# Three sums over partitions in a fused attention and feed-forward layer: matmuls with ones, or transposes that VectorE adds up

## The reference

```python
def _L0_attn_ref(hidden_states, ...):          # hidden_states is the layer norm of x
    x = hidden_states @ up_w.T
    final_gate = hidden_states @ gate_w.T
    shift = silu(causal_conv(x, conv_w) + conv_b)
    q = shift @ q_w.T
    k = shift @ k_w.T
    v = sigmoid(x @ ig_w1.T @ ig_w2.T + ig_b2) * x
    g_gate = softplus(shift @ g_w.T + g_b)
    tau = sigmoid(shift @ tau_w.T + tau_b)
    it_gate = g_gate ** tau
    rt_log = -g_gate * tau
    kn = k / jnp.maximum(jnp.linalg.norm(k, axis=-1, keepdims=True), EPS_K) * it_gate
    o = gla_chunk_scan(q * SCALE, kn, v, rt_log)
    o = o + shift * residual_weight
    xg = o * jax.nn.silu(final_gate)
    rms = jax.lax.rsqrt(jnp.mean(xg * xg, axis=-1, keepdims=True) + NORM_EPS)
    return (xg * rms * norm_weight) @ down_w.T

def _L0_ffn_ref(x, ...):
    h = silu(lin(x, w1)) * lin(x, w2)          # 256 -> 1024
    h = gelu(lin(h, h1))                       # 1024 -> 1024
    h = gelu(lin(h, h2))
    return lin(h, w3)                          # 1024 -> 256
```

## Time and profile before

| | us |
|---|---|
| median of three runs | 1988.01 (1987.57 to 1988.39) |
| span of the profiled execution | 1984.5 |
| PE busy | 1967.8 (99%) |
| DVE busy | 1576.1 (79%) |
| ACT busy | 1258.2 (63%) |
| POOL busy | 68.6 (3%) |

### The profile page before, as it was taken

The page is one execution under the profiler, slowest core; times in us unless marked ns, Lnnn a source line. Parts: engine busy times, 40 slices in busy tenths (PEclk is TensorE's granted clock), DMA queues, the critical chain, the costliest instruction groups (busy, mean ns, idle before and its releaser), DMA issues.

```text
span 1984.5 us, 46801 instructions
## 1 busy us (share of the span) xinstructions
PE 1967.8 (99%) x17508; PEld 1954.0 (98%) x17508; DVE 1576.1 (79%) x4242; ACT 1258.2 (63%) x2495; POOL 68.6 (3%) x104
## 2 busy tenths in 40 slices
PE   7999999999999999999999999999999999999998
PEld 7999999999999999999999999999999999999998
DVE  7787778877788887787877788777888777878777
ACT  5665656666566666566656566665667665666565
POOL 0000000000000000000000000000000000000000
PEclk9999999999999999999999999999999999999999
DMA  8000000000000000000000000000000000000000
GB/s 302 7 12 12 12 7 6 12 12 12 12 1 12 12 12 12 12 1 12 12 12 12 7 6 12 12 12 12 1 12 12 12 12 12 1 12 12 12 7 7
DMA packets 23360, 34.22 MB, mean 17 GB/s; under 512 B 2945, under 2 KB 19713, under 8 KB 23186
## 3 DMA queue, kind: packets, MB, share of 16 engines
q1 hardware_dynamic: 23186, 31.46, 4.7%
HBM read 23.07 MB, written 8.39 MB: 16 GB/s over the span
## 4 chain that ended last, share of the span: by engine, by line
PE 94%; issue 2%; DVE 2%; ACT 1%; SPq 1%; DMA 0%; POOLq 0%; POOL 0%; DVEq 0%; ACTq 0%
PE fb L363 62%; PE ab L363 24%; PE ab L567 2%; PE ab L508 1%; PE ab L433 1%; PE ab L497 1%; PE fb L648 1%; PE ab L560 0%; SPq L271 0%; PE ab L559 0%; DVE hid0l L937 0%; DMA small<-stage_w 0%; ACT raw L801 0%; PE ab L558 0%; SPq L276 0%
## 5 line engine op out<-in xcount | busy, mean ns | idle before, releaser
L363 PE MATMUL fb<-hid1h,wwhole 128*128 128x256 f32 x2048 | 473.7, 279 | 0.2 <-DVE hid1l L854 0.2
L363 PE MATMUL fb<-hid1l,wwhole 128*128 128x256 f32 x2048 | 468.6, 276 | 0.0
L363 PE MATMUL fb<-hid0l,wwhole 128*128 128x256 f32 x2048 | 465.9, 276 | 0.0
L363 PE MATMUL fb<-hid0h,wwhole 128*128 128x256 f32 x2048 | 465.8, 276 | 0.0
L363 PEld LDWEIGHTS fb<-hid1h,wwhole 128*128 128x128 f32 x2048 | 384.7, 188 | 2.6 <-issue 0.4
L363 PEld LDWEIGHTS fb<-hid1l,wwhole 128*128 128x128 f32 x2048 | 384.7, 188 | 0.0
L363 PEld LDWEIGHTS fb<-hid0h,wwhole 128*128 128x128 f32 x2048 | 384.5, 188 | 0.0
L363 PEld LDWEIGHTS fb<-hid0l,wwhole 128*128 128x128 f32 x2048 | 384.4, 188 | 0.0
L801 ACT ACTIVATE raw<-fb,sh_s 128x256 f32<-128x256 f32 x512 | 213.0, 467 | 111.5 <-PE fb L363 110.6
L363 PE MATMUL fb<-xntl,wwhole 128*128 128x256 f32 x1024 | 237.5, 276 | 0.0
L363 PE MATMUL fb<-xnth,wwhole 128*128 128x256 f32 x1024 | 237.5, 276 | 0.0
(11 more groups left out here) (210 smaller groups left out, 4597.7 us busy)
## 6 DMA issues: line engine op xcount, KB each, us to landing
xin<-x SPq DMA_DIRECT2D x32, 256.0 KB, 2.7
out<-xin SPq DMA_DIRECT2D x32, 256.0 KB, 2.2
stage_more<-stage_w SPq DMA_DIRECT2D x6, 512.0 KB, 7.4
sgate<-stage_w SPq DMA_DIRECT2D x4, 512.0 KB, 4.7
shift<-stage_w SPq DMA_DIRECT2D x4, 512.0 KB, 5.2
v<-stage_w SPq DMA_DIRECT2D x4, 512.0 KB, 5.6
raw<-stage_w SPq DMA_DIRECT2D x3, 512.0 KB, 6.3
mixed<-stage_w SPq DMA_DIRECT2D x3, 512.0 KB, 8.6
```

The lines of the kernel that those rows point to most:

```text
L363: mm = pe.matmul(o, a, b, start=start and i == 0, stop=stop and i == len(pairs) - 1)
```

## The change

The matmuls with ones become transposes with the identity that lies in SBUF already. Each result has 128 columns in place of two or one, and DVE adds them up by `tensor_reduce` along the free dimension: for the scores, one reduce of 256 columns in four groups of 64 gives both sums of both chunks; for the mean square, one reduce of 256 columns in two groups of 128. Each reduce signals a semaphore of its own, on which the next DVE instruction waits. The copy of `qk_sum` and the four memsets of `pair_ones` fall away.

```diff
-        pair_ones = sb("pair_ones", [P, NC])
...
-        qk_sum = sb("qk_sum", [P, NC])
+        sums, total = sb("sums", [P, 2 * NC]), sb("total", [P, NC])
+        k_sum, qk_sum = sums[:, 0:NC], sums[:, NC:2 * NC]
...
+        sums_d, total_d = sig("sums_d", 1), sig("total_d", 1)
...
-                pe.matmul(ab[3][:, N:N + NC], t4, pair_ones[:], start=True, stop=True)
-                pe.matmul(ab[3][:, N + NC:N + 2 * NC], qk, pair_ones[:], start=True, stop=True)
+                pe.transpose(ab[3][:, N:N + P], t4, ident_s[:])
+                pe.transpose(ab[3][:, N + P:N + 2 * P], qk, ident_s[:])
...
-                    mm = pe.matmul(fb[1][:, c:c + 1], sqsum[:, c * CH:(c + 1) * CH], ones[:, 0:1], start=True, stop=True)
+                    mm = pe.transpose(fb[1][:, c * P:(c + 1) * P], sqsum[:, c * CH:(c + 1) * CH], ident_s[:])
...
-                    for c in range(NC):
-                        for col in range(NC):
-                            dve.memset(pair_ones[rows(c), col:col + 1], float(c == col))
...
-                dve.tensor_copy(qk_sum[:], ab[3][:, N + NC:N + 2 * NC])
-                dve.tensor_scalar(ssk[:], ab[3][:, N:N + NC], KEPS2, None, ALU.max).then_inc(ss_d.sem, 1)
+                dve.tensor_reduce(sums[:], ab[3][:, N:N + 2 * P].rearrange("p (s k) -> p s k", k=K), mybir.AxisListType.X,
+                                  ALU.add).then_inc(sums_d.sem, 1)
+                dve.wait_ge(sums_d.sem, sums_d.at(me))
+                dve.tensor_scalar(ssk[:], k_sum, KEPS2, None, ALU.max).then_inc(ss_d.sem, 1)
...
-                dve.tensor_scalar(msq[:], fb[1][:, 0:NC], 1.0 / DI, EPS, ALU.mult, ALU.add).then_inc(msq_d.sem, 1)
+                dve.tensor_reduce(total[:], fb[1][:, 0:NC * P].rearrange("p (c k) -> p c k", c=NC), mybir.AxisListType.X,
+                                  ALU.add).then_inc(total_d.sem, 1)
+                dve.wait_ge(total_d.sem, total_d.at(me))
+                dve.tensor_scalar(msq[:], total[:], 1.0 / DI, EPS, ALU.mult, ALU.add).then_inc(msq_d.sem, 1)
```

## The result

The changed kernel takes 1993.19 us (median of 10 runs, 1992.95 to 1994.17), the kernel before 1987.95 us in the same session (1986.91 to 1990.19). The ratio is 1.0027, with a 95% interval of 1.0019 to 1.0036: slower by 5.2 us, where 6.2 us less were forecast. The profiled executions are 7.9 us apart: 1992.4 against 1984.5.

What follows compares the result with a forecast made beforehand. TensorE, busy 99% of the span, was taken as the bound; -4.5 - 1.8 + 0.0 + 0.3 - 0.2 = -6.2 us from the median 1988.01 gave 1981.8 us, 0.31% faster. The range was 1977.5 to 1985.5.

Steps and rivals of the forecast that it cites:

- How near the chain is: VectorE and ScalarE's chain to the fourth `hid1l`, ending 0.14 and 0.21 us before TensorE's k = 6 load; hand-over 0.12.
- the room: Slack at k = 6 of the second hidden layer, capping TensorE's savings since the up projection: 0.02 us (p = 0), 0.09 (p = 1).
- (1): RMS sum at each half's end: two transposes replace two 32-bit matmuls, 0.145 us saved each, 4.5 us in all.
- (2): Two sums at the scores: TensorE 0.12 to 0.22 us earlier, capped by the room to 1.8 us in all.
- (3): VectorE at the scores: reduce of 256 columns takes 0.42 us, `att` is 0.07 late, nothing moves.
- (4): VectorE at the RMS sum: reduce and wait ahead of `msq`, free in 31 halves, +0.34 us once at the end.
- (5): Four memsets at the start go, with TensorE waiting for VectorE's flag there: -0.2 us.
- (B): Rival: VectorE's reduce runs at the strided pace, 0.61 us, delaying the fourth `hid1l`; 1984.6 us, chance 0.15.
- (C): Rival: sign turns, reduce out of PSUM dearer than either row, delaying the fourth `hid1l`; up to 1999.8 us, chance 0.05.
- (D): Rival: a transpose is not cheaper than a one-column matmul on TensorE, nothing saved; 1988.1 us, chance 0.04.
- (A): Rival: the room at k = 6 isn't that small, so all of (2) counts, 5.4 us; 1978.2 us, chance 0.13.
- (E): Rival: TensorE's clock falls to 1.2 GHz around transposes, +14 us at 64 sites; 1996 us, chance 0.02.

Runs made afterwards that it cites:

- e4: Changed kernel with TensorE taking the high parts of k = 6 and 7 in the second hidden layer before waiting for the last low parts; ratio 1.0006 to the kernel before.
- g1: Kernel before with only VectorE's reduce and wait of the score change put ahead of `ssk`; ratio 0.9999 to the kernel before.
- g2: Changed kernel's TensorE work, with VectorE reading two columns at the scores as before, without the sums; ratio 1.0022 to the kernel before.
- e3: Changed kernel with one more transpose, never read, behind the two at the scores; ratio 1.0009 to the kernel before.
- g4: Changed kernel with one more 32-bit matmul of one column behind the two score transposes; ratio 1.0028 to the kernel before.
- f1: Changed kernel with two 64-column matmuls, weights of 16 columns, ahead of the second hidden layer; ratio 0.9992 to the kernel before.
- f4: Kernel before with pairs of small matmuls, weights of 16 columns, ahead of the projections, second hidden layer and third layer; ratio 1.0133, 2014.4 us.
- h1: Kernel before with two short matmuls ahead of the second hidden layer and its high parts taken first at k = 6 and 7; ratio 1.0055.
- h3: Changed kernel with three already met waits added ahead of the second hidden layer; ratio 1.0013 to the kernel before.
- e1: Kernel before with only the RMS sum and its `msq` changed, score sums left as 32-bit matmuls; ratio 0.9989 to the kernel before.
- h4: Changed kernel with the two score transposes moved behind the matmul `kx`; ratio 1.0031 to the kernel before.
- h2: e1 with two short matmuls ahead of the second hidden layer and its high parts taken first at k = 6 and 7; ratio 1.0035.

## Why the prediction was wrong

**What bounds the kernel.** Right: TensorE's own time set the end in every kernel, and the changed kernel has one listed wait of 0.2 us, as in the earlier trace rows. The sentence that failed stands in the same paragraph: "what PE is spared comes off it, as long as no wait opens". It took the time of a matmul as the same whatever goes before it. It isn't: what went before decides between 0.1134 and 0.1178 us for the next 90. The trace of before shows it for whoever takes the same stretch in both halves: the third layer takes 3.63 us in one half and 3.77 in the next. I had read four transposes and three matmuls at the earlier trace rows and taken 0.113 for all, so the spacing of the other matmuls stood at nothing in the sum, and it measured +14.3 us.

**How near the chain is.** Right in p = 0: the wait came, 0.06 us, with a hand-over of 0.11 to 0.12 as in the earlier trace rows. In e4, where the load at k = 6 needn't wait, it begins 0.06 us after the end of the fourth `hid1l`, 0.08 sooner than the 0.14 of the earlier trace rows; 0.08 less the room of 0.02 is the 0.06 of waiting. Wrong in p = 1: no wait came, as the slow spacing had taken 0.09 us before k = 6, and the rest is less than the room. Wrong in its price: I let a wait cost its length, and in ten of the p = 0 halves it costs seven times that, since the spacing behind it is slow. The half of the earlier trace rows could have told me: its 96 matmuls took 11.65 us against 10.88, and the wait was 0.46 of the 0.77. I read the wait's end there and not what followed. (In g1 the same half has the same wait and returns to fast.)

**(1) RMS sum.** Right: 0.34 to 0.22 for the sum, 0.15 and 0.13 with the matmuls behind it, against 0.145.

**(2) Scores.** Right in size, 0.12 where 0.12 to 0.22 was given; the cap at the room was the wrong reason to count little of it. It isn't lost to the wait but bought back at four times its price by the spacing.

**(3) and (4) VectorE.** Right. The reduces take 0.418 and 0.425 us against 0.42, `ssk` follows 0.04 us behind, and the fourth `hid1l` starts right behind its ScalarE input. At the end `msq` starts 0.97 us after the load of the last sum, where it was 1979.32 - 1978.67 = 0.65: 0.32 later against 0.34. The kernel with part (3) alone took 0.9999 of the time before. The note on PSUM that (3) drew from the Trainium skill speaks of matmuls, not of VectorE's reads; the value rested on the rows. **(5)** The preparation's last matmuls start 0.2 us sooner (50.32 for 50.53 us), as forecast.

**The rivals.** (B), (C) and (D) fell with these rows. (A) wanted no wait in either half: it was so in p = 1, for another reason. (E) looked at the clock around the transposes: it is 1.00 in the window from 1000 to 1130 us with all of them in it. The Trainium skill's rule ("TensorE: Matmul & The Clock Gate", Part 4), by which transposes don't count as activity for the clock as matmuls do, changed nothing in the loop here. The clock did fall, but at 51 us, behind the preparation, and in kernels of both kinds. The mechanism that turned the sign was none of the five. The sign turned on a cost of 4.5 ns a matmul; 15106 of the 17508 records are matmuls of that kind, 256 columns on 128 columns of weights.

**The sum.** By the forecast -4.5 - 1.8 + 0.3 - 0.2 = -6.2 us. Measured over the 31 halves of the loop, by the starts of the weight loads: -4.8 at the RMS sum and z and -3.7 at the scores, savings of 8.5; +10.3 in the 96 matmuls of the second hidden layer, +2.0 in the third layer and +2.0 in the down projection, 14.3 for which the forecast had no term; +0.4 elsewhere, most of it a first hidden layer that ran slow once. That is +6.3 in this execution.

## What stays open

What makes a stretch leave the slow spacing was not found. Shown is that the loss comes with TensorE's work and not with VectorE's (g1, g2), that stretches without a wait do the same in nearly all pairs of halves of a kernel, that short work ahead can turn one either way (e3, g4, f1, f4, h1), and that added waits of the sequencer hardly turn it (h3, p = 1). Stretches behind a wait vary from one pair to the next. The first hidden layer is such a stretch in the p = 0 halves: it runs slow in one of them in the changed kernel, in six in e1, three in e3 and every third in h4, and the first load of the projections ahead of it comes 0.165 to 0.183 us behind the load before it, where it comes after 0.110 in the p = 1 halves, a wait of some 0.06 us. It can also reach far: the third layer and the down projection of the p = 0 halves are fast, but for the seven halves whose first hidden layer had run slow (six in e1, one in h1), in all five kernels whose score sums are 32-bit matmuls and that have no added pair ahead of the third layer (before, e1, g1, h1, h2), and slow in all kernels with transposes there, some 20 us of matmuls earlier, whether the second hidden layer between them is fast or slow. That small offsets in time carry this is my reading; no run set an offset on purpose. The starts of the weight loads at the projections speak for it. Where the step to the first load was 0.182 or 0.183 us and the next 0.167 or 0.168, the first hidden layer ran slow in all nine halves (six in e1, two in f1, one in h3); at 0.175 and 0.169 or 0.170 it did in all eight (three in e3, five in h4); at 0.177 or 0.178 and 0.170, as in 14 of the 15 p = 0 halves of the kernel before, in none of 23. That is a pattern of a few ns found across kernels afterwards, and no experiment.

## What to carry to other kernels

Where one engine is busy all the time, time the untouched stretches of its work before and after a change, not only the instructions that are changed: differences of starts along the chain of work show in one view whether equal matmuls still take equal time. Look for that in the trace of before too, by comparing the same stretch in different iterations; if it has two durations, a small change ahead of it can pick the other, and a forecast needs that as a rival of its own. A wait of some 0.05 us in a full stream can cost several times its length, so reordering to avoid it (the high parts first) can be worth more than the wait. Both have to be measured in the kernel at hand: the same reordering with the same short pair, put on the kernel before, cost 14.5 us (h1).

## What the hardware showed that I had not expected

Matmuls of 256 columns with a weight load each have two steady spacings at a granted clock of 1.00, 0.1134 and 0.1178 us, each held for a whole stretch of 128 matmuls in h4. The Trainium skill ("TensorE: Matmul & The Clock Gate", Part 2, Back-to-back issue gap) says that loads and matmuls together set the spacing in such a stream, and gives 256 / 2.4 + 2.5 = 109.2 ns for a matmul alone; both measured values lie above that.

Two 32-bit transposes in a row take 0.22 us with their loads, two 32-bit matmuls with one column 0.34. VectorE adds 256 contiguous 32-bit columns out of PSUM in 0.418 to 0.425 us, while the strided reduce of the earlier trace rows takes 2.0 us for 1024.

In eight of the 18 profiled executions the clock was 1.2 GHz for some 3 us after the preparation, which is 1.6 us of the span; a single profiled pair of these kernels can differ by that without a cause in the code.
